# A four-layer audio tower on one core: the first attention's products spread anew over the gaps between its scores, and GpSimd's norm work put ahead of the first scaling in the nearest-neighbour attention

## What is computed

```python
h = _L0_tok_ref(x)
h = h + _L0_attn_ref(_layernorm(h, axis=-1), L0_attn_Wq, L0_attn_bq, L0_attn_Wk, L0_attn_bk, ...)
...
h = h + _L3_attn_ref(_layernorm(h, axis=-1), L3_attn_Wqkv, L3_attn_Wout, L3_attn_bout)
h = h + _L3_ffn_ref(_layernorm(h, axis=-1), ...)

def _L0_attn_ref(x, Wq, bq, Wk, bk, Wv, bv, Wo, bo):       # 4 heads of 16
    x = jnp.clip(x, -10000.0, 10000.0)
    q = heads(x @ Wq.T + bq)
    k = heads(x @ Wk.T + bk)
    v = heads(x @ Wv.T + bv)
    attn = jax.nn.softmax(jnp.einsum('bhnd,bhmd->bhnm', q, k) * SCALE, axis=-1)
    out = jnp.einsum('bhnm,bhmd->bhnd', attn, v).transpose(0, 2, 1, 3).reshape(B, N, C)
    return out.astype(jnp.bfloat16).astype(jnp.float32) @ Wo.T + bo

def _L3_attn_ref(x, Wqkv, Wout, bout):                     # 8 heads of 64
    adj = _knn_adjacency(x, 32)
    q, k, v = jnp.split(x @ Wqkv, 3, axis=-1)
    dots = jnp.einsum('bhnd,bhmd->bhnm', q, k) * SCALE
    dots = jnp.where(adj[:, None, :, :], dots, -jnp.inf)
    out = jnp.einsum('bhnm,bhmd->bhnd', jax.nn.softmax(dots, axis=-1), v)
    return out.transpose(0, 2, 1, 3).reshape(B, N, HEADS * DIM_HEAD) @ Wout + bout
```

## Time and profile before

| what | us |
|---|---|
| median of 3 runs (4248.11 to 4256.35) | 4252.3 |
| the profiled execution's own time | 4252.19 |
| its span | 4250.4 |
| TensorE busy | 3743.1 |
| VectorE busy | 2833.9 |
| ScalarE busy | 2311.5 |
| GpSimd busy | 1971.4 |
| chain that ended last: TensorE | 53% |
| the same: GpSimd | 15% |
| the same: the scaling L3576 alone | 8% |

### The profile page before, as it was taken

One profiled execution on the slowest core, in us unless ns is written; L12 is line 12 of the kernel. 1 busy time (PEld: TensorE's weight loads), 2 busy tenths in 40 slices (PEclk: granted clock), 3 DMA queues, 4 the chain that ended last, 5 costly groups with the idle time before them and its releaser, 6 DMA issues.

```text
span 4250.4 us, 110086 instructions
## 1 busy us (share of the span) xinstructions
PE 3743.1 (88%) x31697; PEld 2601.1 (61%) x31697; DVE 2833.9 (67%) x9352; ACT 2311.5 (54%) x5677; POOL 1971.4 (46%) x2276
## 2 busy tenths in 40 slices
PE   7488857697999989999898769999999999899999
PEld 7355534386666656666686546666666666555555
DVE  2477747785788744444465878888888887455554
ACT  5455525422444434444343538888888888455555
POOL 0144327674565522222375645555555555334433
PEclk9999977697999989999855879999999999899999
DMA  2111114332111143333111320000000001333332
GB/s 54 36 31 30 30 19 115 96 80 46 37 38 36 46 87 79 79 79 79 44 39 41 66 59 10 12 12 11 11 15 12 11 11 29 67 77 75 75 77 57
DMA packets 465512, 203.02 MB, mean 48 GB/s; under 512 B 435090, under 2 KB 455566, under 8 KB 465170
## 3 DMA queue, kind: packets, MB, share of 16 engines
q1 hardware_dynamic: 465298, 200.65, 20.9%
HBM read 154.67 MB, written 45.91 MB: 47 GB/s over the span
## 4 chain that ended last, share of the span: by engine, by line
PE 53%; issue 16%; POOL 15%; DVE 9%; SPq 2%; DMA 2%; ACT 2%; POOLq 0%; DVEq 0%; ACTq 0%
POOL att_P L3576 8%; PE sw_pH L4191 5%; PE moe_pH L2726 5%; PE sw_pY L4178 5%; PE moe_pY L2749 4%; PE att_pS L982 3%; DVE att_M L1177 3%; PE moe_pH L2730 3%; POOL att_norm_rstd L673 2%; PE moe_pH L2736 2%; PE att_pS L2219 1%; PE att_pO L1044 1%; PE ret_pR L1836 1%; PE att_pO L3039 1%; PE att_pA L3000 1%
## 5 line engine op out<-in xcount | busy, mean ns | idle before, releaser
L3576 POOL TENSOR_TENSOR att_P<-att_P,att_rden 125x498 f32<-125x498 f32 x512 | 515.2, 1018 | 431.7 <-DVE att_rden L3882 430.5
L3773 ACT ACTIVATE att_P<-att_Z,att_nb 125x249 f32<-125x249 f32 x1024 | 499.0, 492 | 10.3 <-DVE att_nb L3894 10.3
L2791 DVE TENSOR_TENSOR moe_hT<-moe_silu,moe_pH 128x498 f32<-128x498 f32 x384 | 258.8, 674 | 312.2 <-ACT moe_silu L2775 312.2
L3894 DVE CUSTOM_DVE_ANT_0 att_Z<-att_pS,att_mask 125x249 f32<-125x249 f32 x1024 | 379.7, 408 | 130.6 <-PE att_pS L3677 127.6
L4239 ACT ACTIVATE sw_hT<-sw_pH,sw_b 128x498 f32<-128x498 f32 x512 | 318.3, 673 | 221.3 <-PE sw_pH L4191 221.3
L2775 ACT ACTIVATE moe_silu<-moe_pH 128x498 f32<-128x498 f32 x384 | 225.3, 587 | 263.0 <-PE moe_pH L2730 177.3
L3780 ACT ACTIVATE att_PTr<-att_pP 125x996 f32<-125x996 f32 x256 | 256.3, 1001 | 158.0 <-PE att_pP L3690 151.0
L2702 POOL TENSOR_TENSOR moe_xe<-moe_share,moe_x 128x1992 f32<-128x1992 f32 x32 | 130.1, 4065 | 430.1 <-DMA moe_share<-mixing 417.5
L4098 POOL TENSOR_TENSOR sw_acc<-sw_acc,sw_Z 128x249 f32<-128x249 f32 x224 | 154.5, 690 | 365.4 <-DVE sw_Z L4318 364.7
L3690 PE MATMUL att_pP<-att_ident,att_P 124*125 124x124 f32 (+1 forms) x2048 | 289.0, 284 | 38.8 <-POOL att_P L3576 38.6
L3690 PEld LDWEIGHTS att_pP<-att_ident,att_P 124*125 124x125 f32 (+1 forms) x2048 | 244.1, 188 | 128.3 <-issue 128.2
(11 more groups left out here) (463 smaller groups left out, 9676.4 us busy)
## 6 DMA issues: line engine op xcount, KB each, us to landing
moe_share<-mixing SPq DMA_DIRECT2D x64, 498.0 KB
sw_share<-mixing SPq DMA_DIRECT2D x64, 498.0 KB, 5.5
ffn_W<-in_ffn_pairs SPq DMA_DIRECT2D x64, 192.0 KB, 2.4
att_F<-h_stream SPq DMA_DIRECT2D x192, 62.5 KB
att_X<-h_stream SPq DMA_DIRECT2D x192, 62.5 KB
h_stream<-att_H SPq DMA_DIRECT2D x64, 62.5 KB
ffn_F<-h_stream SPq DMA_DIRECT2D x64, 62.5 KB
ret_F<-h_stream SPq DMA_DIRECT2D x64, 62.5 KB
```

The source lines that it names most:

```text
L2791: v.tensor_tensor(hT[:, u, k, :, :], sl[:, k % 3, :, :], pH[:, k % 3, :, T:2 * T], ALU.mult).then_inc(*hid_ready.one())
L3576: g.tensor_tensor(own, own, bc(rden[:, j % 2, c, :], T), ALU.mult).then_inc(*scaled.one())
L3773: ins = a.activation(P[:, r, c, t, :], Z[:, r, c, t, :], ACT.Exp, scale=-1.0, bias=nb[:, r, c, t:t + 1], accum_out=den[:, r, c, t:t + 1])
L3894: ins = v.tensor_tensor_reduce(Z[:, s % 2, c, t, :], pS[:, c, t * T:(t + 1) * T], mask[:, u, s // HP, t, :], -1.0, -TAKEN, ALU.add, ALU.mi ...
```

## The change

No instruction's work changes, only its place. In the first attention TensorE's gaps become: y, mean, turn, xn (gap 1); probabilities times V, turn (gap 2); OT's transposition, q and k (gap 3); turn back, V (gap 4). The steps of the other engines follow. H1 moves from step 0 of its wave to step 2, the mean of a pair is computed one slot group behind y of the next pair (`sum_up`), and takes the wait for H1. In the nearest-neighbour attention GpSimd's scalings move from places 0 and 3 to places 2 and 3, and the centring to step 1, in front of the squares.

```diff
 # stage_attention0, GpSimd
             def pre(n, u, step):
-                if step == 3:
+                if step == 1:
                     g.wait_ge(*xn_ready.before(n))
                     norm.center(g, n, g4(F[:, u % 2, :, :, :]))
+                if step == 6:
+                    norm.power(g, n)
             def proj(n, u, step):
                 if step == 0:
-                    norm.power(g, n)
...
             def ends(n, u, step):
-                if step == 2:
+                if step == 4:
                     g.wait_ge(*mean_done.before(n))
                     tail.center(g, n, g4(H1[:, u % 2, :, :, :]))
                     tail.square(g, n)
-                if step == 6:
+                if step == 7:
                     tail.power(g, n)
 # TensorE
             def proj(n, u, step):
-                if step == 3:
+                if step == 1:
                     pe.wait_ge(*xn_ready.after(n))
                     pe.wait_ge(*xT_ready.before(n))
-                    if since(n, 3):
-                        pe.wait_ge(*OT_ready.after(n - 3))
+                    if since(n, 4):
+                        pe.wait_ge(*OT_ready.after(n - 4))
...
             def post(n, u, step):
-                if step == 1:
+                if step == 3:
                     pe.wait_ge(*exp_ready.after(n))
                     pe.wait_ge(*OT_ready.before(n))
-                    pe.wait_ge(*xT_ready.after(upto(n + 2)))
+                    pe.wait_ge(*xT_ready.after(upto(n + 3)))
...
-                if step == 3:
+                if step == 5:
                     pe.wait_ge(*OT_ready.after(n))
...
-                if step == 5:
+                if step == 7:
                     pe.wait_ge(*ob_ready.after(n))
...
-                if step == 7:
+            def sum_up(n):
+                pe.wait_ge(*tail.powered.after(n))
...
+                ins.then_inc(*mean_done.one())
+            def ends(n, u, step):
+                if step == 1:
                     pe.wait_ge(*oT_ready.after(n))
...
                     ins.then_inc(*y_done.one())
+                    if since(n, 1):
+                        sum_up(n - 1)
 # ScalarE
             def pre(n, u, step):
-                if step == 5:
+                if step == 3:
                     norm.square_scalar(a, n)
...
             def post(n, u, step):
-                if step == 1:
+                if step == 3:
                     a.wait_ge(*o_done.after(n))
...
-                if step == 5:
+                if step == 7:
                     a.wait_ge(*back.after(n))
...
+            def ends(n, u, step):
+                if step == 3 and since(n, 1):
+                    a.wait_ge(*h_ready.after(n))
+                    take(n - 1)
 # VectorE
             def pre(n, u, step):
-                if step == 3:
+                if step == 1:
                     v.wait_ge(*loaded.after(n, u % 2))
                     norm.sums(v, n, g4(F[:, u % 2, :, :, :]))
-                if step == 7:
+                if step == 5:
                     norm.spread(v, n, 1e-5)
             def proj(n, u, step):
-                if step == 3:
+                if step == 1:
                     v.wait_ge(*xT_done.after(n))
...
             def post(n, u, step):
-                if step == 3:
+                if step == 5:
                     v.wait_ge(*turned.after(n))
...
             def ends(n, u, step):
-                if step == 0:
+                if step == 2:
                     v.wait_ge(*y_done.after(n))
+                    if since(n, 1):
+                        v.wait_ge(*mean_done.after(n - 1))
...
-                if step == 1:
+                if step == 3:
                     v.wait_ge(*h_ready.after(n))
                     tail.sums(v, n, g4(H1[:, u % 2, :, :, :]))
-                if step == 5:
+                if step == 6:
                     tail.spread(v, n, 1e-5)
 # stage_attention3, GpSimd
             def pre(n, u, x):
                 s, place = divmod(x, PLACES)
-                if s == 0 and place == 5:
+                if s == 1 and place == 1:
                     g.wait_ge(*xn_ready.before(n))
                     norm.center(g, n, g4(F[:, u, :, :, :]))
-                if s == 1 and place == 1:
                     norm.square(g, n)
...
             def main(n, u, x):
-                if place in (0, 3) and s >= 1:
-                    scale(n, s - 1, place // 3)
+                if place in (2, 3) and s >= 1:
+                    scale(n, s - 1, place - 2)
             def post(n, u, x):
-                if place in (0, 3) and s == 0:
-                    scale(n, STEPS - 1, place // 3)
+                if place in (2, 3) and s == 0:
+                    scale(n, STEPS - 1, place - 2)
```

More of the change, by code:

```diff
@@ L1075, in post @@
                     ins.then_inc(*y_done.one())
+                    if since(n, 1):
+                        sum_up(n - 1)
             def sums(n, u, step):
-                if step == 1:
-                    pe.wait_ge(*tail.powered.after(n))
+                if step == 1 and isinstance(n, int) and n == PAIRS - 1:
+                    pe.wait_ge(*h_ready.after(n))
                     pe.wait_ge(*mean_ready.before(n))
-                    pe.wait_ge(*h_ready.after(upto(n + 1)))
-                    st.held(pe)
-                    for t in range(2):
-                        ins = pe.matmul(pX[:, 256:258],
-                                        tail.xc[0:ROWS[t], 2 * t:2 * t + 2, :].rearrange("p g c -> p (g c)"),
-                                        tail.rstd[0:ROWS[t], 2 * t:2 * t + 2], start=(t == 0), stop=(t == 1))
-                    ins.then_inc(*mean_done.one())
-            waves(pe, (nothing, proj, front, main, post, nothing, sums), STEPS, PERIOD)
+                    sum_up(n)
+            waves(pe, (nothing, proj, front, main, post, ends, sums), STEPS, PERIOD)
         @block.scalar
@@ L1122, in post, with take @@
                         *OT_ready.one())
-                if step == 5:
+                if step == 7:
                     a.wait_ge(*back.after(n))
                     a.activation(oT[:, :], pX[:, 0:T], ACT.Copy).then_inc(*oT_ready.one())
-            def sums(n, u, step):
-                if step == 1:
-                    a.wait_ge(*mean_done.after(n))
-                    a.activation(mean[:, bass.ds(n * 2, 2)], pX[:, 256:258], ACT.Copy,
-                                 scale=1.0 / T).then_inc(*mean_ready.one())
-            waves(a, (pre, proj, nothing, main, post, nothing, sums), STEPS, PERIOD)
+            def take(n):
+                a.wait_ge(*mean_done.after(n))
+                a.activation(mean[:, bass.ds(n * 2, 2)], pX[:, 256:258], ACT.Copy,
+                             scale=1.0 / T).then_inc(*mean_ready.one())
+            def ends(n, u, step):
+                if step == 3 and since(n, 1):
+                    a.wait_ge(*h_ready.after(n))
+                    take(n - 1)
+            def sums(n, u, step):
+                if step == 3 and isinstance(n, int) and n == PAIRS - 1:
+                    take(n)
+            waves(a, (pre, proj, nothing, main, post, ends, sums), STEPS, PERIOD)
         @block.vector
```

5 lines of the change are left out of this document (added).

## The result

The changed kernel takes **4175.1 us** (median of 4 runs, 4172.75 to 4181.31), the kernel before 4253.5 (4 runs): a ratio of 0.9822, 95% interval 0.9807 to 0.9837. So 78 us went where I had forecast 60 (4192) and had drawn the range to 4172. Its profiled execution has a span of 4171.6 us.

The account below looks back on a forecast made before the run. Nothing is full in the first attention, where TensorE waits for VectorE's maxima; the nearest-neighbour attention is nearly full on TensorE, which waits for GpSimd's scalings. 25 + 35 = 60 us off 4252.19 gives 4192; range 4172 to 4224.

Parts of the forecast that it names:

- The first attention: Moving work between TensorE's gaps shortens a wave from 12.67 to 11.85 us; 25 us over thirty waves.
- with the spacings of rows 3 and 4: First attention: one new wave laid out by hand using TensorE and VectorE spacings from the earlier profile; wave 11.85 us.
- The bound I gave as the most: First attention: with TensorE and the floor alone, a wave takes 11.35 us, gaining at most 1.3 a wave or 40 us.
- VectorE has no idle time before maxima 1 and 3: Sign in the first attention: VectorE's queue is late there, by 0.35 us (covered) and 0.45 us (exposed).
- TensorE waits over 1 us before slot 0: Sign in the first attention: TensorE idles over 1 us before each new wave's first scores slot, in 30 waves.
- The nearest-neighbour attention: Norm operations ahead of GpSimd's paired scalings remove 35 of TensorE's 37.3 us of waits; ends 0 and 38.
- to a few: Sign in the nearest-neighbour attention: TensorE's 37.3 us of waits for GpSimd's scalings shrink to a few us.
- A: First attention: GpSimd's power holds VectorE's tail-variance tensor_scalar; wave 12.4 us, gain only 8 us, total 4209; chance 0.07.
- B: First attention gives nothing: VectorE's tight order in gaps 1 and 3 adds 0.8 us of waits; 4217; chance 0.12.
- C: Nearest-neighbour attention gives nothing: norm operations in front wait for VectorE and hold both scalings; 4227; chance 0.07.
- D: Both stages: no net change, B and C together or waits left as they are; 4252; chance 0.05.
- E: First attention slower: GpSimd's adding bo to X waits for X's load; landing at 18 us gives 4325; chance 0.04.

Follow-up runs that it names:

- the two runs: Changed kernel with GpSimd's nearest-neighbour norm power between a step's two scalings: 4199.7 us; changed kernel with its square between them instead: 4193.3 us (one run).
- the version with the variance in gap 2: Changed kernel, but in the first attention ScalarE squares in step 2 and VectorE takes that variance in step 3, ahead of the third maxima: 4170.5 us.
- two versions 16 us apart by their times: Changed kernel with variance in gap 2, 4170.5 us; the same with a four-wave nearest-neighbour loop body on VectorE and GpSimd alone, 4154.6 us.

## Why the prediction was right

The direction, both mechanisms and the range held; both terms were too small, the first by more. That the range held is in part luck: 78.4 us were gained, and the most that I had allowed was 40 + 38 = 78, which is 4174; the 4172 that I gave as its lower end is 2 us below that sum. I had put 25 us where I myself had 40 as the bound.

**The first attention** (25 us forecast; 40 by the last mean, 42 by the run with this edit alone). My layout against the trace, interval by interval:

| from slot | forecast | measured |
|---|---|---|
| 0 to 1 | 2.78 | 2.61 |
| 1 to 2 | 3.33 | 3.24 |
| 2 to 3 | 2.69 | 2.72 |
| 3 to 0 | 3.05 | 2.77 |
| wave | 11.85 | 11.34 |

The order of events is as laid out: maxima 1 late and covered, maxima 3 late and exposed, TensorE with no wait but before slot 0. The step that failed is "with the spacings of rows 3 and 4". Those I took from places where the instruction behind waited for another engine, or where I reckoned a small one at its whole length, and used them for ones that wait for nothing. Behind slot 2's maxima I had 0.67 + 0.65 + 0.65 to maxima 3; measured are 0.63 + 0.52 + 0.55 = 1.70 (373.07 to 374.77), which is the 0.28 of the last line but for 0.01. Of a variance the reduction takes 0.44 to its tensor_scalar, as before; the next instruction starts 0.08 to 0.10 behind that one, where my 0.65 had 0.21 for it. H to the maxima took 0.34, not 0.44, and the four instructions ahead of H 0.06 less than reckoned, so maxima 1 are 0.20 late, not 0.35; the turn behind the product with the values then waits for nothing, which is the 0.09 of the second line. And the mean product takes TensorE 0.36 us from start to start and not 0.50, the distance it had behind a wait and ahead of another product (which of the two made it is not shown); that, with the turn and xn at 0.25 and 0.41, is the first line. 0.51 us by 30 waves is 15 us, all of the missing gain of this stage. The bound I gave as the most, 11.35 and 40 us, is what came; the runs with the added reduction, products and turn say why: only 0.16 us of VectorE is in the wave, and it stands in gap 3. "VectorE has no idle time before maxima 1 and 3" and "TensorE waits over 1 us before slot 0": the first is right; the second came as 0.57. Of the difference 0.28 is maxima 3, which were not as late; the rest is TensorE's own work in gap 4 and its wait of 0.17 there for ScalarE's kT, 4.9 us in 29 waves, which I had costed at nothing. It is covered by the wait for the maxima, so it cost nothing.

**The nearest-neighbour attention** (35 us forecast; 38.5 by the trace, 37.8 alone). The 37.3 us of waits went to 1.1 ("to a few"), a plain wave takes 31.15 (said: 31.5), and the 0.4 us of room ahead of the first scalings are in the rows. The forecast held tenths back for the waves behind the turn of the loop; they were not needed, and the 38 that I gave as the most was passed by 0.5. The waits fell by 36.2; where the stage's other 2 us come from is not shown. That the gain is nearly all these waits, and how it splits into 0.3 for the squares and 0.9 for the power, the two runs bear out at 0.41 and 0.85.

**The rivals.** *A* (the power holds the tensor_scalar) fell: 0.17 us, 0.28 us into a power, in gap 3. The Trainium skill (SBUF — State Buffer, "Who interferes with whom") has whoever starts first hold the shared ports for the whole instruction. For a power this case's trace does not show it; for squares it does, by the 0.48 us of the version with the variance in gap 2. That version lost by it part of what it was to gain. *B* (the first attention gives nothing) fell by the run with that edit alone, 42.1 us, and *C* by the other, 37.8. *D*, no net change, went with them. *E* (GpSimd waits for the load of X): GpSimd's adding of bo to X stands right behind the centring in the changed kernel's rows, 380.50 behind 379.93, with no wait, so the load had landed; what a late load would cost was not tried.

## What to carry to other kernels

Lay a wave out by hand before moving work between gaps, but take a spacing from two instructions that stand to each other as they will in the new order, with no idle time between them: behind the same small reduction VectorE's next instruction came after 0.33 us where it did not need the result and after 0.44 where it did, and behind a tensor_scalar of 0.17 us it came after 0.08 to 0.10. 15 of this stage's 40 us hung on such tenths. When an engine must do side work between two pieces that another waits for as a pair, put it ahead of the pair, into the wait for its input; it cost TensorE 0.85 and 0.41 us a time between them, next to nothing ahead. And ask of each gap by itself who sets it: 0.33 us of VectorE cost 0.30, 0.08 or nothing, depending on the gap. Last, compare runs by their ratio to the kernel that ran beside them, or by rows: two versions 16 us apart by their times were 11 apart by both of these.

## What the runs showed of the hardware

- **The turn of a loop** costs an engine with a long body 1.8 to 2.9 us, and one with a short body a few tenths at most: VectorE 1.95 to 2.27 us with two waves in the body and 1.95 to 2.20 with four; TensorE and ScalarE show no such stall with two, and 2.7 (16.4 in 6) and 2.0 us with four. What is long differs by engine. Counted in the traces, with what the sequencers do, a body that stands has 453 instructions on VectorE (two waves), 562 on ScalarE and 2236 on TensorE (four); one that does not has 282 on ScalarE and 1122 on TensorE (two). Where between these the limits lie no run shows. Making the body longer on just the engine that already paid halved the number of its turns and saved 11 us; on the others it bought them a stall that they did not have. What in the machine stands behind it the profile does not show ("issue").
- **A tensor_scalar of 125x4** took 0.17 us beside GpSimd's power of 125x4, and 0.48 beside GpSimd's squares of 125x256, ending 0.03 us after them. In all fourteen traces together 691 of them started inside such a power, and each took 0.17; 81 started inside such squares, took 0.42 to 0.62 and ended 0.02 to 0.03 us after them. Which of GpSimd's instructions it is beside decides, not that there is one.
